# A graph layer kernel: a reordered head, and ring chunks taken in turn with others in the third unit

## The chip, the cores and the metric

One core of one Trainium2 chip runs the kernel. The metric is the device time of one execution in microseconds (us), as the median of several runs.

## The reference

There are 256 nodes with 1024 features and 8448 edges (66 tiles of 128). What matters of it:

```
h = relu(layernorm(x))
feat = concat(h[src], h[dst])              # 8448 x 2048
e = relu(feat @ W_kind + b_kind)           # kind hh: tile 0; oo: tiles 1 to 5; ho: the other 60
logit = e @ W_a + b_a
alpha = softmax of logit over the edges with the same dst
z = segment_sum(alpha * h[src], dst)
x1 = x + relu(concat(h, z) @ W_hn or W_on + bias)     # rows 0..63 use hn, the others on
out = x1 + relu(layernorm(x1)) @ W.T + l1_bias        # W scattered from edge_weight at (src, dst)
```

## The kernel before

**Units.** For the ho edges the kernel doesn't multiply 8448 rows: it makes the tables p_ho = h @ top and q_ho = h @ bottom (256 rows each), stores them in HBM and gathers one row of each per edge. The work on TensorE (PE) is in units of 8 chunks; a chunk is 128 rows of a weight matrix (512 KB). Units 0 and 1 (p_ho, q_ho) are the split units: each chunk is rounded to a high half Wh (ScalarE, ACT, L423) and a remainder Wl (VectorE, DVE, L633), h transposed likewise to hTh (ACT, L455) and hTl (DVE, L639), and `split_chunk` (L858 to L873) makes three products per row tile and column half: hTh by Wh, hTh by Wl, hTl by Wh, 12 matmuls per chunk. Then comes the hh unit (L972 to L998): 16 chunks against hsT, the gathered rows of tile 0. The other units (tables oo, then on and hn) are jobs (L1000 on) of one chunk or a pair each, dealt out between the lots by PACE.

**Lots.** Edge tiles go in lots of mostly 3. Per tile, POOL gathers a row block of p into Gp (12 slots) and one of q into Gq (8 slots); DVE adds them (`total`, L682), makes two onehots (L673, L675) and the logit (L686); ACT makes weight products RW (L490) and logit products RL (L500); PE counts edges (psC in psB, and psW) and places logits (psA), both at L918. The onehot ring has 9 slots, so DVE's tenth onehot after the early ones waits for the first placed tile (L670).

**The head.** SP loads x in two tiles (L258), the ids, and five weight chunks. DVE takes the statistics, ACT makes h (L414) for each row tile and then issues the store of h_rows (L417), from which tile 0's rows are gathered (L364). PE waits for the constants, then transposes h (L845). It holds hTh and hTl, Wh and Wl of the chunk complete before it starts a chunk's first product (L858, with the wait for s_hTl before even chunks). POOL clears `zero` last of its memsets (L348).

**Order of the weights.** SP issues ring loads (W, 5 slots) in order: while q-5 is in the split units, load q waits for its remainder; afterwards it waits on the chunk that used the slot (`uses_before`, L95). The first 11 chunks of the hh unit do not lie in the ring but in buffers that are free then: pre_f (3), pre_l (2, the place of RL), Gq slots 4 to 7, and two parts of T. Its chunks 11 to 15 lie in the five ring slots and are used last. So the ring's next load (q = 21) waits for the twelfth hh chunk, and the gathers into Gq slots 4 to 7 wait for the chunks there (L389).

```
            for c in range(2):
                for k in range(KC):
                    n = c * KC + k
                    q = SPLIT + n - PRE
```

Of the kernel before, what the change touches and what calls it, by code (L numbers as in the profile page):

```python
# [44 lines left out]
HALVES = 4  # L45
NP = 12
# [14 lines left out]
TOPS = SPLIT + HH - PRE + PLAIN  # L61
CHUNKS = TOPS + 2 * KC
# [32 lines left out]
def uses_before(q):  # L95

    gone = q - WSLOTS
    if gone < SPLIT:
        return gone + 1
    return gone + PRE + 1 if gone < TOPS else TOPS + PRE + (gone - TOPS) // 2 + 1  # L100


def gnn_block(nc, x, edge_ids, edge_w, weights, bias_rows, w_a, b_a, l1_bias, out):
# [13 lines left out]
    with ctx:  # L117
# [95 lines left out]
        s_x = [sem(f"x_in{t}") for t in range(NT)]  # L213
# [42 lines left out]
        def _(sp):  # L256
            for t in range(NT):
                sp.dma_start(xs[:, t, :], by_tile(x)[:, t, :]).then_inc(s_x[t], 16)  # L258
# [82 lines left out]
        def _(pool):  # L341
            nc.gpsimd.memset(epst[:, :], EPS).then_inc(s_eps, 1)
            nc.gpsimd.memset(minus[:, :], -1.0)
# [4 lines left out]
            nc.gpsimd.memset(zero[:, :], 0.0)  # L348
# [9 lines left out]
                                    pattern=[[-1, BIASES]], channel_multiplier=1).then_inc(s_const, 1)  # L358
            pool.wait_ge(s_ids, 16)
# [47 lines left out]
        def _(act):  # L407
            act.wait_ge(s_eps, 1)
            nc.scalar.activation(warm[:, :], epst[:, :], ACT.Sqrt)
            for t in range(NT):  # L410
# [41 lines left out]
            for b in range(4):  # L452
                highs(b, b + 1)
# [40 lines left out]
            def logit_product(g, i, half, val):  # L494
# [3 lines left out]
                elif half == 0:  # L498
                    act.wait_ge(s_wused, SPLIT + PRE_HEAD)
# [96 lines left out]
        def _(dve):  # L596
# [11 lines left out]
            def half_stats(t, b):  # L608
                chain(nc.vector.bn_stats(st[:, t, b, :], xs[:, t, b * HALF:(b + 1) * HALF]))
# [10 lines left out]
            dve.wait_ge(s_x[0], 16)  # L620
# [3 lines left out]
            dve.wait_ge(s_x[1], 16)  # L624
# [4 lines left out]
            norm(1)  # L629

            def low(q):
                dve.wait_ge(s_hi, q + 1)
# [205 lines left out]
        def _(pe):  # L838
            pe.wait_ge(s_const, 1)
            for t in range(NT):  # L840
                pe.wait_ge(s_h, t + 1)
                for b in range(4):
                    for i in range(2):
# [41 lines left out]
            for k in range(KC):  # L885
                if k % 2 == 0:
                    pe.wait_ge(s_hTl, k // 2 + 1)
# [81 lines left out]
            for c in range(2):  # L969
                for k in range(KC):  # L970
                    n = c * KC + k
                    q = SPLIT + n - PRE  # L972
                    if n < PRE:
                        pe.wait_ge(s_pre[n], 16)
                    else:
                        chunk_in(q)
                    rows = pre[n] if n < PRE else W[:, q % WSLOTS, :]
                    for half in range(2):
                        last = nc.tensor.matmul(psG[:, half, :], hsT[:, c, k, :], rows[:, half * HALF:(half + 1) * HALF],  # L979
                                                start=False, stop=c == 1 and k == KC - 1, skip_group_check=True)  # L980
                    last.then_inc(s_wused, 1)
                    i = n - 2
                    if 0 <= i < len(EARLY):
                        count(i, EARLY[i:i + 1])
                    elif i == 6:
                        lot_count(0)
                    elif i == 8:
                        lot_count(1)
                    elif i == 9:
                        lot_place(0)  # L990
# [194 lines left out]
```

## Time and profile before

| | us |
|---|---|
| median of 3 runs (326.26 to 327.69) | 326.42 |
| the profiled execution's own time | 328.05 |
| its span, first to last instruction | 326.2 |
| PE busy | 304.4 (93%) |
| DVE busy | 254.3 (78%) |
| ACT busy | 175.9 (54%) |
| POOL busy | 155.1 (48%) |
| moved by DMA | 122.06 MB, mean 374 GB/s |
| granted TensorE clock, mean | 0.989 |

Busy PE is modelled from starts and counts overlapping instructions once; "issue" is time in which an engine waits for nothing that the profile shows; "remote" is a releaser that the profile could not name. A float32 matmul of 128x512 appears as two instructions.

### The profile page before, as it was taken

What the parts mean: (1) busy time and instruction counts of PE and PEld (TensorE: products, weight loads), DVE (VectorE), ACT (ScalarE), POOL (GpSimd) and SP (SyncE); (2) the same over time, 40 slices, a digit from 0 to 9 for tenths busy, and PEclk for the clock granted to TensorE, in tenths of its full rate; (3) what the DMA queues carried; (4) which work ended last, traced back from release to release, by engine and by line L of the source; (5) the groups of instructions that cost most, each with busy time, mean ns of one, the idle gap of its engine ahead of it and who ended that gap; (6) DMA issues with size and microseconds to landing.
All of it is one profiled execution on the core that took longest, in us unless ns stands there. A gap on an engine that the chain in (4) does not pass through costs nothing.

```text
span 326.2 us, 4198 instructions
## 1 busy us (share of the span) xinstructions
PE 304.4 (93%) x1381; PEld 194.7 (60%) x1381; DVE 254.3 (78%) x446; ACT 175.9 (54%) x437; POOL 155.1 (48%) x148
## 2 busy tenths in 40 slices
PE   0899999999958999999999999999989989999995
PEld 0687688755634756665766675575645554456543
DVE  4657437303992998999989999999999999986444
ACT  3873451372461586277874465576438398562202
POOL 3040048307784877657766658578777720000000
PEclk9999999999996999999999999999999999999999
DMA  7999999998999999999999999999999999999304
GB/s 263 404 403 410 407 377 395 409 418 324 346 390 370 384 413 408 409 410 408 411 417 408 409 410 410 405 418 410 409 408 411 409 407 409 406 407 410 110 0 129
DMA packets 34425, 122.06 MB, mean 374 GB/s; under 512 B 4058, under 2 KB 4570, under 8 KB 34404
## 3 DMA queue, kind: packets, MB, share of 16 engines
q0 software_dynamic: 19008, 69.21, 53.7%
q1 hardware_dynamic: 14004, 47.34, 37.5%
q10 hardware_dynamic: 1392, 5.24, 3.9%
q8 instruction: 11, 0.18, 0.2%
q14 instruction: 10, 0.08, 0.1%
HBM read 115.49 MB, written 6.29 MB: 373 GB/s over the span
## 4 chain that ended last, share of the span: by engine, by line
PE 59%; DVE 25%; ACT 8%; issue 5%; another core or an unknown queue 2%; DMA 1%; ACTq 0%; DVEq 0%
PE psG L868 13%; PE psG L1010 11%; PE psG L979 9%; DVE Gp L686 7%; DVE Gp L682 7%; PE psA L918 6%; PE psW L918 6%; PE psB L918 3%; PE psG L1032 3%; ACT RL L500 3%; DVE ohd L675 2%; PE psG L1087 2%; DVE inv_few L728 2%; PE psG L1040 2%
## 5 line engine op out<-in xcount | busy, mean ns | idle before, releaser
L379 POOL DMA_INDIRECT Gp<-p_ho,ids x60 | 66.7, 1112 | 55.2 <-DMA p_ho<-T 24.2
L682 DVE TENSOR_TENSOR Gp<-Gp,Gq 128x1024 f32<-128x1024 f32 x65 | 79.2, 1218 | 15.9 <-DMA Gq<-q_ho,ids 15.9
L393 POOL DMA_INDIRECT Gq<-q_ho,ids x60 | 70.3, 1172 | 34.1 <-issue 17.4
L1010 PE MATMUL psG<-W,hT 128*128 128x512 f32 x192 | 84.9, 592 | 0.0
L686 DVE SCALAR_TENSOR_TENSOR Gp<-Gp,wa 128x1024 f32<-128x1024 f32 x65 | 79.1, 1217 | 0.4
L1010 PEld LDWEIGHTS psG<-W,hT 128*128 128x128 f32 x192 | 35.3, 190 | 39.1 <-issue 39.1
L490 ACT ACTIVATE RW<-ohs,ewh 128x256 fp32r<-128x256 f32 x66 | 33.2, 504 | 41.9 <-DVE ohs L673 29.3
L918 PE MATMUL psW<-RW,ohd 128*128 128x256 f32 x264 | 44.4, 290 | 0.0
L918 PE MATMUL psA<-RL,ohd 128*128 128x256 f32 x240 | 36.2, 289 | 7.6 <-issue 4.8
L918 PEld LDWEIGHTS psA<-RL,ohd 128*128 128x128 f32 x240 | 31.1, 190 | 13.5 <-issue 7.2
L918 PEld LDWEIGHTS psW<-RW,ohd 128*128 128x128 f32 x264 | 36.3, 189 | 3.0 <-issue 2.9
L633 DVE TENSOR_TENSOR Wl<-W,Wh 128x1024 fp32r<-128x1024 f32 x16 | 19.6, 1223 | 20.2 <-ACT Wh L423 20.2
L673 DVE TENSOR_SCALAR ohs<-iota,idf 128x256 fp32r<-128x256 f32 x72 | 26.3, 365 | 9.7 <-remote 8.5
L500 ACT ACTIVATE RL<-ohs,lg 128x256 fp32r<-128x256 f32 x66 | 32.9, 499 | 0.0
L500 ACT ACTIVATE RL<-ohs,lgl 128x256 fp32r<-128x256 f32 x66 | 32.7, 495 | 0.1
L490 ACT ACTIVATE RW<-ohs,ewl 128x256 fp32r<-128x256 f32 x66 | 32.7, 496 | 0.0
L918 PE MATMUL psB<-ohs,ohd 128*128 128x256 f32 x132 | 31.8, 328 | 0.0
L918 PEld LDWEIGHTS psB<-ohs,ohd 128*128 128x128 f32 x132 | 20.9, 189 | 10.4 <-issue 10.0
L675 DVE TENSOR_SCALAR ohd<-iota,idf 128x256 fp32r<-128x256 f32 x72 | 25.6, 356 | 0.0
L423 ACT CAST Wh<-W 128x1024 fp32r<-128x1024 f32 x16 | 16.8, 1052 | 16.0 <-PE psG L868 15.0
L868 PE MATMUL psG<-Wh,hTh 128*128 128x512 f32 x64 | 20.5, 402 | 1.4 <-DVE hTl L639 1.4
L868 PE MATMUL psG<-Wl,hTh 128*128 128x512 f32 x64 | 19.8, 391 | 0.0
(180 smaller groups left out, 360.5 us busy)
## 6 DMA issues: line engine op xcount, KB each, us to landing
W<-weights SPq DMA_DIRECT2D x61, 512.0 KB, 13.9
Gp<-weights SPq DMA_DIRECT2D x8, 512.0 KB, 10.1
Gq<-weights SPq DMA_DIRECT2D x4, 512.0 KB, 10.8
pre_f<-weights SPq DMA_DIRECT2D x3, 512.0 KB, 6.7
xs<-x SPq DMA_DIRECT2D x2, 512.0 KB, 3.7
h_rows<-h ACTq DMA_DIRECT2D x1, 1024.0 KB, 6.5
pre_l<-weights SPq DMA_DIRECT2D x2, 512.0 KB, 9.3
p_ho<-T ACTq DMA_DIRECT2D x2, 512.0 KB, 6.5
```

The source lines that it names most:

```text
L379: nc.gpsimd.indirect_dma_start(out=Gp[:, i % NP, :], out_offset=None, in_=p_oo if t <= OO_TILES else p_ho, in_offset=bass.IndirectOffsetOn ...
L393: nc.gpsimd.indirect_dma_start(out=Gq[:, i % NQ, :], out_offset=None, in_=q_oo if t <= OO_TILES else q_ho, in_offset=bass.IndirectOffsetOn ...
L490: last = nc.scalar.activation(RW[:, w % WRING, half, :], ohs[:, (first + i) % RING, :].bitcast(f32), ACT.Copy, scale=val[:, t:t + 1].bitca ...
L500: return nc.scalar.activation(RL[:, n % LRING, half, :], ohs[:, (ENTRY[g] + i) % RING, :].bitcast(f32), ACT.Copy, scale=val[:, g % 2, i:i ...
L673: nc.vector.tensor_scalar(ohs[:, n % RING, :], iota[:, :], idf[:, tile, 0:1], None, ALU.is_equal).then_inc(s_ohs, 1)
L675: nc.vector.tensor_scalar(ohd[:, n % RING, :], iota[:, :], idf[:, tile, 1:2], None, ALU.is_equal).then_inc(s_ohd, 1)
L682: nc.vector.tensor_tensor(Gp[:, i % NP, :], Gp[:, i % NP, :], Gq[:, i % NQ, :], ALU.add).then_inc(s_sum, 1)
L686: nc.vector.scalar_tensor_tensor(out=Gp[:, i % NP, :], in0=Gp[:, i % NP, :], scalar=0.0, in1=wa[:, :], op0=ALU.max, op1=ALU.mult, accum_ou ...
L868: ins = nc.tensor.matmul(psG[:, 2 * t + half, :], lhs[:, k, cols], rhs[:, s, half * HALF:(half + 1) * HALF], start=not opened and k == 0 a ...
L918: ins = nc.tensor.matmul(bank[:, c, :], ohd[:, slot, c * P:(c + 1) * P], m, start=False, stop=False, skip_group_check=True)
L979: last = nc.tensor.matmul(psG[:, half, :], hsT[:, c, k, :], rows[:, half * HALF:(half + 1) * HALF], start=False, stop=c == 1 and k == KC - ...
L1010: last = nc.tensor.matmul(psG[:, 2 * t + half, :], hT[:, k, t * P:(t + 1) * P], W[:, s, half * HALF:(half + 1) * HALF], start=u != 1 and k ...
```

## The change

It changes six things.

1. x is loaded as four DMAs of half a row tile each, and each statistics instruction waits for its half alone.
2. PE runs 12 matmuls of zeros (WARM) into psG before it waits for the constants; POOL clears `zero` right after its first memset, for that.
3. h of the second row tile: ACT makes columns 0 to 511, DVE the others in two instructions. The store of h_rows moves from ACT's queue to SP's, behind the first loads and the bias rows, with waits for both parts.
4. The high halves of weight chunks 0 and 1 are made by POOL (POOL_HIGHS), before its cast of the ids; ACT makes those from 2 on.
5. `split_chunk` waits for Wh and hTh at its start, for Wl before the first product with it, and for hTl before the first with that.
6. The hh unit takes its chunks as 3, 4, 11, 5, 12, 6, 13, 7, 14, 8, 15, 9, 10, 0, 1, 2. The waits of the ring, of RL, of Gq slots 4 to 7 and of `few_counts` are put on the matching steps. Counts and the first placement stay at the same steps of the unit.

```diff
+HH_ORDER = [3, 4] + [11, 5, 12, 6, 13, 7, 14, 8, 15] + [9, 10] + [0, 1, 2]
+HH_USED = {n: SPLIT + i + 1 for i, n in enumerate(HH_ORDER)}
...
+    if gone < SPLIT + HH - PRE:
+        return HH_USED[PRE + gone - SPLIT]
...
             for t in range(NT):
-                sp.dma_start(xs[:, t, :], by_tile(x)[:, t, :]).then_inc(s_x[t], 16)
+                for half in range(2):
+                    cols = slice(half * HALF, (half + 1) * HALF)
+                    sp.dma_start(xs[:, t, cols], by_tile(x)[:, t, cols]).then_inc(s_x[t][half], 16)
...
             sp.dma_start(bar[:, :], b_a.broadcast_to((P, 1))).then_inc(s_small, 16)
+            sp.wait_ge(s_h, NT)
+            sp.wait_ge(s_hd, 1)
+            sp.dma_start(by_tile(h_rows), h[:, :, :]).then_inc(s_hst, 16)
...
+            nc.gpsimd.memset(zero[:, :], 0.0).then_inc(s_zero, 1)
...
+            for q in range(POOL_HIGHS):
+                pool.wait_ge(s_w[q], 16)
+                nc.gpsimd.tensor_copy(Wh[:, q, :], W[:, q, :]).then_inc(s_hip, 1)
             pool.wait_ge(s_ids, 16)
...
-                    pool.wait_ge(s_wused, SPLIT + PRE_HEAD + i - HALVES + 1)
+                    pool.wait_ge(s_wused, HH_USED[PRE_HEAD + i - HALVES])
...
-                nc.scalar.activation(h[:, t, :], xs[:, t, :], ACT.Relu, bias=nb[:, t:t + 1],
+                cols = slice(0, (D, HALF)[t])
+                nc.scalar.activation(h[:, t, cols], xs[:, t, cols], ACT.Relu, bias=nb[:, t:t + 1],
                                      scale=rs[:, t:t + 1]).then_inc(s_h, 1)
-            act.wait_ge(s_h, NT)
-            act.dma_start(by_tile(h_rows), h[:, :, :]).then_inc(s_hst, 16)
...
-                highs(b, b + 1)
+                if b >= POOL_HIGHS:
+                    high(b)
...
-                    act.wait_ge(s_wused, SPLIT + PRE_HEAD)
+                    act.wait_ge(s_wused, max(HH_USED[3], HH_USED[4]))
...
+            chain(nc.vector.tensor_scalar(h[:, 1, HALF:D], xs[:, 1, HALF:D], rs[:, 1:2], nb[:, 1:2], ALU.mult, ALU.add))
+            nc.vector.tensor_scalar(h[:, 1, HALF:D], h[:, 1, HALF:D], 0.0, None, ALU.max).then_inc(s_hd, 1)
...
-                dve.wait_ge(s_wused, SPLIT + 2)
+                dve.wait_ge(s_wused, SPLIT + HH)
...
+            pe.wait_ge(s_zero, 1)
+            for _ in range(WARM):
+                nc.tensor.matmul(psG[:, 0, :], zero[:, 0:P], zero[:, :], start=True, stop=True, skip_group_check=True)
             pe.wait_ge(s_const, 1)
...
+                    if t == NT - 1 and b == 2:
+                        pe.wait_ge(s_hd, 1)
...
-                pe.wait_ge(s_lo, q + 1)
+                if q < POOL_HIGHS:
+                    pe.wait_ge(s_hip, q + 1)
+                else:
+                    pe.wait_ge(s_hi, q - POOL_HIGHS + 1)
+                pe.wait_ge(s_hTc, k // 2 + 1)
...
+                        if t == 0 and n == 1:
+                            pe.wait_ge(s_lo, q + 1)
+                        elif t == 0 and n == 2:
+                            pe.wait_ge(s_hTl, k // 2 + 1)
...
-            for c in range(2):
-                for k in range(KC):
-                    n = c * KC + k
-                    q = SPLIT + n - PRE
+            for step, n in enumerate(HH_ORDER):
+                c, k = divmod(n, KC)
+                q = SPLIT + n - PRE
```

## Rows read from the trace of the kernel before

**Rows 1.** The page: busy share of each engine, and DMA in 40 slices of the span.

```profile
PE 304.4 (93%) x1381; PEld 194.7 (60%) x1381; DVE 254.3 (78%) x446; ACT 175.9 (54%) x437; POOL 155.1 (48%) x148
...
DMA  7999999998999999999999999999999999999304
```

**Rows 2.** Timeline of the head (start us, us, engine, line, what), to the last h.

```profile
0.74 0.86 SPq L258 DMA_DIRECT2D xs<-x  x2
...
4.01 1.42 DVE L609 BATCH_NORM_STATS2 st<-xs 128x6 f32<-128x512 f32 x2 [4.01 <-DMA xs<-x]
...
6.66 1.24 ACT L414 ACTIVATE h<-xs,nb,rs 128x1024 f32<-128x1024 f32 x1 [0.66 <-DVE nb L617]
...
8.51 1.24 ACT L414 ACTIVATE h<-xs,nb,rs 128x1024 f32<-128x1024 f32 x1 [0.42 <-DVE nb L617]
```

**Rows 3.** Timeline, the work of the first weight chunk and of the first hT bank.

```profile
10.22 1.05 ACT L423 CAST Wh<-W 128x1024 fp32r<-128x1024 f32 x1 [0.47 <-ACT h L414]
...
11.17 0.58 ACT L455 CAST hTh<-psB 128x512 fp32r<-128x512 f32 x1
...
11.30 1.22 DVE L633 TENSOR_TENSOR Wl<-W,Wh 128x1024 fp32r<-128x1024 f32 x1 [2.82 <-ACT Wh L423]
...
12.44 0.68 DVE L639 TENSOR_TENSOR hTl<-psB,hTh 128x512 fp32r<-128x512 f32 x1
```

**Rows 4.** The chain that ended last: first products of the split unit.

```profile
13.18 13.91 PE psG L868 x60
```

**Rows 5.** Groups by line in 0 to 45 us: the nearest prices (mean ns).

```profile
L845 PE MATMUL psB<-ident,h 128*128 128x128 f32 x8 | 2.2, 431 | 8.0 <-ACT h L414 8.0
...
L908 PE MATMUL psB<-ident,hs 128*128 128x128 f32 x8 | 1.2, 271 | 0.0
...
L347 POOL MEMSET brow<- 64x1024 f32 x1 | 1.0, 956 | 0.0
...
L360 POOL CAST idf<-ids 128x132 f32<-128x132 int32 x1 | 0.3, 293 | 2.5 <-DMA ids<-edge_ids 2.5
```

**Rows 6.** Windows: busy time of each engine, granted clock, DMA share, GB/s.

```profile
0.00:7.00 7.00, 0.00 (x0) 0.00 (x0) 2.85 (x7) 2.12 (x4) 3.11 (x16) 1.00 0.75 241
...
75.00:80.00 5.00, 5.00 (x20) 2.68 (x18) 1.09 (x1) 0.47 (x2) 3.78 (x5) 1.00 0.79 309
...
85.00:115.00 30.00, 24.99 (x108) 16.21 (x107) 23.45 (x42) 15.36 (x44) 20.56 (x19) 0.89 1.01 376
...
130.00:262.00 132.00, 129.90 (x588) 81.35 (x586) 129.40 (x226) 77.65 (x216) 92.13 (x80) 1.00 1.03 410
```

**Rows 7.** Timeline of POOL and SP between the two gather waves.

```profile
73.40 0.94 POOL L393 DMA_INDIRECT Gq<-q_ho,ids  x1 [12.35 <-DMA q_ho<-T]
...
83.02 1.00 POOL L393 DMA_INDIRECT Gq<-q_ho,ids  x1 [0.41 <-PE psG L979]
...
103.51 6.29 SPq L262 DMA_DIRECT2D W<-weights  x5
```

**Rows 8.** The chain that ended last, hh unit, and where PE crawls.

```profile
70.09 1.72 PE psG L979 x4
...
71.81 0.47 PE psW L918 x4
...
92.69 0.28 PE psA L918
...
101.09 8.36 PE psG L979 x16
```

**Rows 9.** Timeline of DVE: its first sum, and its longest idle time after it.

```profile
78.91 1.23 DVE L682 TENSOR_TENSOR Gp<-Gp,Gq 128x1024 f32<-128x1024 f32 x1 [15.88 <-DMA Gq<-q_ho,ids]
...
103.65 0.35 DVE L673 TENSOR_SCALAR ohs<-iota,idf 128x256 fp32r<-128x256 f32 x1 [6.55 <-remote]
```

**Rows 10.** The end: DVE's wait for x (timeline), and the chain beside it.

```profile
307.01 0.69 DVE L806 SCALAR_TENSOR_TENSOR x<-psG,x 128x512 f32<-128x512 f32 x1 [2.51 <-DMA x<-x]
...
308.40 5.15 PE psG L1087 x24
```

More of the change, by code:

```diff
@@ L45 @@
 HALVES = 4
+POOL_HIGHS = 2
+WARM = 12
 NP = 12
@@ L61 @@
 TOPS = SPLIT + HH - PRE + PLAIN
+HH_ORDER = [3, 4] + [11, 5, 12, 6, 13, 7, 14, 8, 15] + [9, 10] + [0, 1, 2]
+HH_USED = {n: SPLIT + i + 1 for i, n in enumerate(HH_ORDER)}
+assert sorted(HH_ORDER) == list(range(HH))
 CHUNKS = TOPS + 2 * KC
@@ L211, in gnn_block @@
         hT_banks = [psB[:, 0, :], psB[:, 1, :], whole(psA), whole(psW)]
-        s_x = [sem(f"x_in{t}") for t in range(NT)]
+        s_x = [[sem(f"x_in{t}{half}") for half in range(2)] for t in range(NT)]
+        s_zero, s_hip, s_hd = sem("zero_made"), sem("first_w_high_made"), sem("h_last_half_made")
         s_ids, s_ew, s_wa, s_small = map(sem, ("ids_in", "ew_in", "wa_in", "small_in"))
@@ L347, in _ @@
             nc.gpsimd.memset(brow[:, :], 0.0).then_inc(s_pool, 1)
-            nc.gpsimd.memset(zero[:, :], 0.0)
             nc.gpsimd.iota(iota[:, :], pattern=[[1, N]], base=0, channel_multiplier=0,
@@ L608, in half_stats @@
             def half_stats(t, b):
+                dve.wait_ge(s_x[t][b], 16)
                 chain(nc.vector.bn_stats(st[:, t, b, :], xs[:, t, b * HALF:(b + 1) * HALF]))
@@ L618, in norm @@
                                                op0=ALU.mult, op1=ALU.mult).then_inc(s_nb, 1)
-            dve.wait_ge(s_x[0], 16)
             half_stats(0, 0)
@@ L623, in _ @@
             variance(0)
-            dve.wait_ge(s_x[1], 16)
             half_stats(1, 0)
@@ L629, in _ @@
             norm(1)
+            dve.wait_ge(s_nb, NT)
+            chain(nc.vector.tensor_scalar(h[:, 1, HALF:D], xs[:, 1, HALF:D], rs[:, 1:2], nb[:, 1:2], ALU.mult, ALU.add))
+            nc.vector.tensor_scalar(h[:, 1, HALF:D], h[:, 1, HALF:D], 0.0, None, ALU.max).then_inc(s_hd, 1)
             def low(q):
-                dve.wait_ge(s_hi, q + 1)
+                if q < POOL_HIGHS:
+                    dve.wait_ge(s_hip, q + 1)
+                else:
+                    dve.wait_ge(s_hi, q - POOL_HIGHS + 1)
                 nc.vector.tensor_tensor(Wl[:, q % HALVES, :], W[:, q % WSLOTS, :], Wh[:, q % HALVES, :].bitcast(f32),
@@ L860, in split_chunk @@
             def split_chunk(q, k, opened):
-                pe.wait_ge(s_lo, q + 1)
+                if q < POOL_HIGHS:
+                    pe.wait_ge(s_hip, q + 1)
+                else:
+                    pe.wait_ge(s_hi, q - POOL_HIGHS + 1)
+                pe.wait_ge(s_hTc, k // 2 + 1)
                 s = q % HALVES
@@ L885, in _ @@
             for k in range(KC):
-                if k % 2 == 0:
-                    pe.wait_ge(s_hTl, k // 2 + 1)
                 split_chunk(k, k, False)
@@ L968, in _ @@
             bias(1, everyone, 0, 1)
-            for c in range(2):
-                for k in range(KC):
-                    n = c * KC + k
-                    q = SPLIT + n - PRE
[L973 to L990, printed above, removed]
+            for step, n in enumerate(HH_ORDER):
+                c, k = divmod(n, KC)
+                q = SPLIT + n - PRE
+                if n < PRE:
+                    pe.wait_ge(s_pre[n], 16)
+                else:
+                    chunk_in(q)
+                rows = pre[n] if n < PRE else W[:, q % WSLOTS, :]
+                for half in range(2):
+                    last = nc.tensor.matmul(psG[:, half, :], hsT[:, c, k, :], rows[:, half * HALF:(half + 1) * HALF],
+                                            start=False, stop=step == HH - 1, skip_group_check=True)
+                last.then_inc(s_wused, 1)
+                i = step - 2
+                if 0 <= i < len(EARLY):
+                    count(i, EARLY[i:i + 1])
+                elif i == 6:
+                    lot_count(0)
+                elif i == 8:
+                    lot_count(1)
+                elif i == 9:
+                    lot_place(0)
             def job(j):
```

## The prediction

> **What bounds the kernel now.** I read the page first. PE is busy 93% of the span and the DMA engines stand at 9 tenths in nearly every slice [rows 1]: two resources are full at once, and DVE is the third. The windows say it more closely: from 130 to 262 us PE works 129.9 of 132 us, DVE 129.4, and DMA has a share of 1.03 at 410 GB/s [rows 6]. In that stretch nothing can be gained by reordering; a gain must come from before it, and it must bring all three forward.
>
> Before it there are three losses. First, the head: h is made from 6.66 and 8.51 us on [rows 2], and the first real product starts at 13.18 [rows 4]. Second, PE crawls from 92.69 to 101.09: the 12 matmuls of the first placement take 8.4 us [rows 8], and DVE stands idle for 6.55 us until 103.65 because its onehot needs the first placed tile [rows 9]; the ring's next load also goes out only at 103.51 [rows 7]. The profile names no wait of PE there. Third, DMA runs dry at 75 to 80 us (share 0.79, 309 GB/s), and while only gathers are queued it gives 376 GB/s in 85 to 115 us rather than 410 [rows 6].
>
> **x in four.** The whole first tile lands 4.01 - 0.74 = 3.3 us after its issue [rows 2]. Its first half holds 256 KB, 0.64 us less of transfer at 410 GB/s [rows 6], so DVE's first statistics start 0.6 us sooner and the second follows; h0 then starts near 6.0 instead of 6.66. Two more issues of 0.43 us each (0.86 us for two [rows 2]) push the first weight loads on SP back by 0.9 us. That I cost at nothing: the x, ids and W0 bytes (1.64 MB) need until 7.0 us at the 241 GB/s of the window 0 to 7 [rows 6], so W0 stands in the DMA queue anyway; without that cover it is 0.9 us.
>
> **h split between ACT and DVE.** Second tile: ACT's 1.24 us [rows 2] become about 0.65; DVE takes two 128x512 instructions. There is no such row; bounds are 0.3 us (a quarter of the 1.22 us for 128x1024 with two inputs [rows 3]) and 0.7 us (the 0.68 of hTl [rows 3]); I take 0.45, as one input is read. So h is whole at about 7.85 + 0.95 = 8.8 instead of 8.51 + 1.24 = 9.75.
>
> **The warm-up.** The early transposes take 431 ns, later ones of the same shape 271 ns [rows 5]: PE runs at the lower of its two levels (1.2 GHz) after having done nothing for 8 us, though the clock column shows 1.00. Twelve matmuls of 512 columns, at twice the 13.91 / 60 = 0.23 us of the full level [rows 4], fill 5.6 us from about 1.5 us on, to 7.1: before h0 is there (7.2), so they delay nothing. The 8 transposes of the second tile then need about 1 us rather than 2. First bank ready at 8.8, hTh of it (0.58 [rows 3]) at 9.4.
>
> **POOL makes two high halves.** POOL has no 128x1024 cast in the trace. Below: 0.96 us, its memset of 1024 columns; above: 0.293 x 1024 / 132 = 2.3 us, its only cast scaled up [rows 5]. I take 1.6, the cast with some 0.1 us of fixed time taken off. From W0's landing at about 7.2 they run to 8.8 and 10.4. ACT loses two casts of 1.05 us that stood ahead of hTh [rows 3].
>
> **Products of high halves first.** PE starts at 9.5 with hTh by Wh. Then Wl of chunk 0 (DVE, 1.22) is ready at 8.9 + 1.2 = 10.1, hTl (0.68) at 10.8 [rows 3]. Two of the 12 matmuls are done by then and perhaps two more; the other 8 take 8 x 0.23 = 1.9 us: chunk 0 ends at 12.7. Before it ends at 13.18 + 12 x 0.23 = 15.9. Gain 3.2 us.
>
> The rows show no POOL read beside a DVE instruction with two inputs in SBUF. Bounds: no delay, or DVE's first Wl waits for the end of POOL's second copy (10.4) and chunk 0 ends at 14.2, gain 1.7 us. The Trainium skill, page "SBUF — State Buffer", section "Who interferes with whom", says that a VectorE instruction with two SBUF inputs and a GpSimd instruction that reads SBUF block each other, whichever starts first holding the port; by it the lower gain, 1.7 us, is the one to take. POOL's second copy begins at the same moment as Wl 0 can, so either may win; I take 3.0 us and keep 1.7 for the range.
>
> Later chunks keep it. DVE needs 1.22 + 0.68 = 1.9 us per chunk and bank, PE 2.76; W lands in time, for 4 chunks of Wh lie ahead of PE. The h_rows store on SP holds up only loads that need Wl 0 anyway, and its gathered rows are first used in unit 1. POOL's later cast of the ids is wanted only by the onehots, which stand on DVE behind all sixteen remainders. Were that cover gone, it would be POOL's 3.2 us.
>
> **The hh order.** No instruction is added. A chunk costs 1.72 us and a tile's counts 0.47 [rows 8]. The unit starts near 64.3 - 3.0 = 61.3. The ring's slots come free after steps 3, 5, 7, 9 and 11, so five loads (2.6 MB, 6.4 us of DMA) go out between 67 and 86 us instead of from 103.51 on [rows 7]. They fill the hole at 75 to 80 (0.21 x 5 = 1.05 us). Against it: Gq slot 7 comes free with step 10, at 61.3 + 10 x 1.72 + 6 x 0.47 + 2.1 = 83.4 (2.1: three tiles of lot 0, each 0.47 for psW and half as much for psC), while POOL issues that gather at 83.02 now [rows 7]. POOL's queue holds behind it all later gathers, which therefore go out as now, 0.4 us later; DVE comes to that tile only 7 tiles after its first sum, each with 1.23 for the sum, the like for the logit and 0.35 for a onehot, pipelined near 2.8: about 98. So that costs nothing. Job 0 will find its chunk landed, but PE shows no wait there now. So I cost this part at 0 on the chain, with 1 us gained by DMA.
>
> **The sum.** PE reaches the first placement at 92.7 - 3.0 = 89.7. The logits it needs come from DVE, whose first sum stands at 78.91 [rows 9] even if the gathers do not come sooner; lot 0's products are then ready from 89 on (three tiles and 1.6 us on ACT). If the crawl keeps its 8.4 us, DVE's wait, the next lots and everything until the end go 3.0 us earlier: 328.05 - 3.0 = 325.05 for the profiled execution. Its own time is 1.63 us over the median, so the median becomes 326.42 - 3.0 = 323.4. Does DMA allow it? x lands at 307.01 now; its readers must be done when the hn rows end after 308.40 + 5.15 = 313.55 [rows 10], and new_rows with its statistics needs twice 0.69 us: 5.1 us of slack, plus the 1 us from the hole. Three fit.
>
> **Rivals.**
> (a) **The crawl goes.** It may depend on what else stands in the queues at 92 to 103 us: only gathers are there then, and after the change the ring loads are done and DVE is as far as before. If it goes, DVE gains its 6.55 us [rows 9] and PE 3.0 and most of the 8.4; DMA's slack of 6.1 us then decides: 326.4 - 6.1 = 320.3. For it: no row gives the crawl a cause inside PE. Against: nothing in the edit touches it.
> (b) **DMA takes the head's gain.** DMA is full from 2 us on, and the first q gather had to wait for the q_ho store in it until 73.40 [rows 7]; the bytes ahead of it are the same, plus two ring loads. If the later stages hang on DMA at 410 GB/s, only the 1 us of the hole is won: 325.5, within noise of 326.4. For it: share 1.03 throughout. Against: DVE never waits for a gather after its first.
> (c) **The edit does less than it says:** port or slow POOL copies leave 1.7 us or none: 325.
> (d) **Slower.** The five ring loads now run ahead of the first q gathers. They can delay DVE's first sum by their 6.4 us, and slot 7's wait may add to it. The idle 6.55 us at 97 to 103.65 absorb that; it decides only once the first sum comes after 78.91 + 6.55 = 85.5 us. With another 2 us of wait for slot 7 the time is 326.4 + 2 = 328.4.
>
> **How the numbers follow.** Forecast, 323.4: 0.42, own range 322 to 324.9. (a) 0.23. (b) and (c) together 0.23. (d) 0.12. A difference of 0.5% (1.6 us) is about what a measurement of this kernel tells from none. Faster: 0.41 of the forecast, (a), and 0.02 of (c): 0.66. Same: 0.22. Slower: 0.12. The range reaches from 318.8, where (a) also wins DMA's whole slack and its rate beside gathers, to 327.2, which leaves out most of (d).
>
> **What would show it.** First L868 matmul at 9.5 us and not 13.18; chunk 0's end near 12.7 (14.2 if the port blocks); Wl 0 right beside POOL's copies. The hh unit starting near 61.3. Ring loads between 67 and 86 us and a window 75 to 80 with a share near 1. POOL's eighth q gather near 83.4. DVE's first sum at 76 to 79. The crawl still there, 3 us earlier, and DVE's release near 100.6. I am wrong if PE is at 61.3 but DVE's release is not before 103, or if the last x lands after 312.

## The result, and the profile after

| | us, median (lowest to highest) | runs |
|---|---|---|
| before | 326.07 (324.97 to 328.35) | 13 |
| after | 324.21 (322.88 to 327.01) | 13 |

The ratio is 0.9946, with a 95% interval of 0.9922 to 0.9970: faster by about 0.5%, at the edge of what the prediction called measurable. By medians that is 1.9 us, and the forecast was 3.0. The profiled execution took 323.78 us with a span of 322.0, 4.3 us less than that of before (328.05 and 326.2). So the two traces show more than the medians; the first experiment says why. In the table of the experiments the ratios and their intervals leave out runs in a slower state (two of r9, three of r10, two of r11, one of r12 and one of the kernel before on that chip), while the medians hold all runs.

The page of after, with the engines' busy time, the DMA engines' tenths, and the share of each engine in the chain that ended last:

```profile
PE 308.8 (96%) x1388; PEld 195.8 (61%) x1393; DVE 256.2 (80%) x448; ACT 174.2 (54%) x435; POOL 156.7 (49%) x150
...
DMA  6999999999999999999999999999999999999604
...
DMA 29%; PE 21%; DVE 20%; POOL 18%; issue 9%; ACT 2%; SPq 1%; ACTq 0%; DVEq 0%
```

The same line of the page of before, the chain:

```profile
PE 59%; DVE 25%; ACT 8%; issue 5%; another core or an unknown queue 2%; DMA 1%; ACTq 0%; DVEq 0%
```

PE was 59% of the chain in that profile, and now DMA has the largest part. The edit did not do this: a second profile of the kernel before (r1 below) has PE 26%, DMA 24%, DVE 20%.

The timeline of the head, after:

```profile
3.45 0.69 DVE L628 BATCH_NORM_STATS2 st<-xs 128x6 f32<-128x512 f32 x1 [3.45 <-DMA xs<-x]
...
6.48 1.24 ACT L433 ACTIVATE h<-xs,nb,rs 128x1024 f32<-128x1024 f32 x1 [0.72 <-DVE nb L636]
...
8.91 0.43 DVE L649 TENSOR_SCALAR h<-h 128x512 f32<-128x512 f32 x1
9.07 3.33 POOL L376 CAST Wh<-W 128x1024 fp32r<-128x1024 f32 x2 [5.53 <-DMA W<-weights]
...
10.26 1.22 DVE L656 TENSOR_TENSOR Wl<-W,Wh 128x1024 fp32r<-128x1024 f32 x1 [0.93 <-POOL Wh L376]
...
10.40 0.70 PE L904 MATMUL psG<-Wh,hTh 128*128 128x512 f32 x2
11.41 0.68 DVE L662 TENSOR_TENSOR hTl<-psB,hTh 128x512 fp32r<-128x512 f32 x1
```

h of the first tile starts at 6.48 instead of 6.66 [rows 2], and the first product at 10.40 instead of 13.18 [rows 4]. Chunk 0 ends near 14.1; the prediction had worked out 15.9 for before. W0 is late: POOL waits for it until 9.07. POOL's two copies stand as one line of 3.33 us, 9.07 to 12.40, and DVE's Wl 0 lies inside it, from 10.26 to 11.48. A copy took 1.04 us in later kernels where it began before DVE's instruction (r8, r12); so the second of this pair was held up.

Windows of after (columns as in [rows 6]):

```profile
34.00:41.00 7.00, 6.05 (x19) 4.19 (x19) 2.35 (x3) 1.66 (x3) 0.00 (x0) 0.76 1.03 414
37.00:38.00 1.00, 1.00 (x4) 0.81 (x3) 0.88 (x1) 0.09 (x1) 0.00 (x0) 0.50 1.02 406
75.00:80.00 5.00, 5.00 (x18) 2.67 (x18) 0.70 (x1) 0.57 (x2) 3.78 (x5) 1.00 1.02 364
85.00:115.00 30.00, 29.75 (x135) 18.94 (x134) 30.00 (x54) 20.83 (x59) 22.04 (x20) 1.00 0.99 372
130.00:262.00 132.00, 128.24 (x577) 80.96 (x578) 125.48 (x219) 82.55 (x227) 94.22 (x81) 0.99 1.03 410
```

The stretch 75 to 80 is fuller than before (364 GB/s instead of 309), and 130 to 262 runs at the same 410 GB/s [rows 6]. PE's clock is lost at the seam of the two split units, at its lower level (0.50, 1.2 GHz) from 37 to 38. Before, PE has 1.00 there. It stood idle at 34 to 36.3, in bits (0.38 us waiting for DVE and 0.57 us for ACT), before the clock fell. Of the eight other profiles with the new head two lose it there too (r5 at 0.76 and r12 at 0.86 in 34 to 41 us).

The first and the eighth q gather on POOL, after:

```profile
73.33 0.93 POOL L411 DMA_INDIRECT Gq<-q_ho,ids  x1 [13.43 <-DMA q_ho<-T]
...
87.16 1.44 POOL L411 DMA_INDIRECT Gq<-q_ho,ids  x1 [4.17 <-PE psG L1012]
```

The first starts as before (73.40 [rows 7]), the eighth 4.1 us later than before, after an idle 4.17 us.

PE after, at the start of the hh unit and at the first placement:

```profile
64.30 3.70 PE L1012 MATMUL psG<-pre_l,hsT 128*128 128x512 f32 x8
...
91.87 1.98 PE L952 MATMUL psA<-RL,ohd 128*128 128x256 f32 x12
```

The 12 matmuls of the first placement take 1.98 us. The crawl of [rows 8] is gone, and so is DVE's idle 6.55 us of [rows 9]. In its place, DVE after:

```profile
79.30 1.22 DVE L705 TENSOR_TENSOR Gp<-Gp,Gq 128x1024 f32<-128x1024 f32 x1 [16.72 <-DMA Gq<-q_ho,ids]
...
159.64 1.22 DVE L705 TENSOR_TENSOR Gp<-Gp,Gq 128x1024 f32<-128x1024 f32 x1 [1.44 <-DMA Gq<-q_ho,ids]
...
286.22 1.22 DVE L705 TENSOR_TENSOR Gp<-Gp,Gq 128x1024 f32<-128x1024 f32 x1
...
306.01 0.69 DVE L829 SCALAR_TENSOR_TENSOR x<-psG,x 128x512 f32<-128x512 f32 x1 [5.79 <-DMA x<-x]
```

DVE waits for gathers here, at nine of its sums between 159 and 279 us; one of them is shown. In the first profile of before it waited only at its first. The sum of the last tile stands at 286.22, against 287.72 there. DVE had been 8.2 us ahead of that trace at its seventeenth sum (124.63 against 132.81), and at the last it was 1.5. Most of the 8.2 us is the crawl of that one profile, not the edit: in r1 the seventeenth sum stands at 125.88, 1.3 us behind after, and DVE waits for gathers as well. So time won back from the crawl does not arrive at the last sum, because DVE then waits for rows. The last x lands for DVE's use at 306.01, before the 312 that was to show the prediction wrong.

### The profile page after: what moved, and what is told of

Same layout as the page of the kernel before. It is cut to its first block, busy times and chain, and to the rows that moved or that the text cites. A ratio compares the mean times of both kernels' runs of the same rounds, so it can differ in the third digit from the quotient of the medians.

```text
span 322.0 us, 4235 instructions
## 1 busy us (share of the span) xinstructions
PE 308.8 (96%) x1388; PEld 195.8 (61%) x1393; DVE 256.2 (80%) x448; ACT 174.2 (54%) x435; POOL 156.7 (49%) x150
## 4 chain that ended last, share of the span: by engine, by line
DMA 29%; PE 21%; DVE 20%; POOL 18%; issue 9%; ACT 2%; SPq 1%; ACTq 0%; DVEq 0%
DMA Gq<-q_ho,ids 14%; POOL Gp L397 10%; POOL Gq L411 8%; PE psG L904 7%; DMA W<-weights 7%; DMA Gq<-q_oo,ids 7%; DVE Gp L705 5%; PE psG L1012 5%; DVE Gp L709 5%; DVE inv_few L751 2%; PE psG L1120 2%; PE psW L952 1%; DVE ohd L698 1%; PE psG L1115 1%; DVE Wl L656 1%
## 5 line engine op out<-in xcount | busy, mean ns | idle before, releaser
L397 POOL DMA_INDIRECT Gp<-p_ho,ids x60 | 70.6, 1177 | 47.5 <-DMA p_ho<-T 24.2
L411 POOL DMA_INDIRECT Gq<-q_ho,ids x60 | 66.0, 1100 | 40.4 <-issue 16.8
L1043 PEld LDWEIGHTS psG<-W,hT 128*128 128x128 f32 x192 | 35.7, 192 | 39.6 <-issue 39.1
L952 PE MATMUL psA<-RL,ohd 128*128 128x256 f32 x240 | 37.0, 296 | 3.6 <-ACT RL L518 2.7
L952 PEld LDWEIGHTS psW<-RW,ohd 128*128 128x128 f32 x264 | 36.3, 189 | 2.9 <-issue 2.9
L440 ACT CAST Wh<-W 128x1024 fp32r<-128x1024 f32 x14 | 14.6, 1054 | 18.1 <-PE psG L904 8.9
L904 PE MATMUL psG<-Wh,hTh 128*128 128x512 f32 x64 | 21.3, 415 | 0.1
```

Of the source, the lines that this page charges most:

```text
L397: nc.gpsimd.indirect_dma_start(out=Gp[:, i % NP, :], out_offset=None, in_=p_oo if t <= OO_TILES else p_ho, in_offset=bass.IndirectOffsetOn ...
L411: nc.gpsimd.indirect_dma_start(out=Gq[:, i % NQ, :], out_offset=None, in_=q_oo if t <= OO_TILES else q_ho, in_offset=bass.IndirectOffsetOn ...
L904: ins = nc.tensor.matmul(psG[:, 2 * t + half, :], lhs[:, k, cols], rhs[:, s, half * HALF:(half + 1) * HALF], start=not opened and k == 0 a ...
L952: ins = nc.tensor.matmul(bank[:, c, :], ohd[:, slot, c * P:(c + 1) * P], m, start=False, stop=False, skip_group_check=True)
L1043: last = nc.tensor.matmul(psG[:, 2 * t + half, :], hT[:, k, t * P:(t + 1) * P], W[:, s, half * HALF:(half + 1) * HALF], start=u != 1 and k ...
```

## The experiments

All were timed beside the kernel before on the same chip. Runs 1 to 4 share one chip (before: 326.25, 35 runs), 5 to 8 a second (325.93, 11 runs), 9 to 12 a third (326.85, 35 runs).

| kernel | median us | ratio to before (95%) | hh unit starts | last sum | span |
|---|---|---|---|---|---|
| r1 before, again | 325.87 | 0.9995 (0.9969 to 1.0022) | 65.91 | 288.03 | 323.8 |
| r2 head only | 324.47 | 0.9955 (0.9926 to 0.9983) | 63.25 | 285.39 | 321.1 |
| r3 order only | 325.36 | 0.9979 (0.9948 to 1.0009) | 66.43 | 289.55 | 325.3 |
| r4 busy gap | 324.36 | 0.9961 (0.9933 to 0.9988) | 64.42 | 288.77 | 324.5 |
| r5 after, more bytes | 329.64 | 1.0112 (1.0080 to 1.0143) | 64.64 | 294.14 | 329.9 |
| r6 before, more bytes | 331.71 | 1.0181 (1.0147 to 1.0216) | 64.39 | 292.42 | 328.2 |
| r7 after, half rows | 330.03 | 1.0116 (1.0079 to 1.0153) | 62.98 | 292.40 | 328.1 |
| r8 slots first | 321.94 | 0.9882 (0.9856 to 0.9909) | 62.34 | 284.21 | 320.0 |
| r9 slots, old head | 326.50 | 0.9972 (0.9937 to 1.0008) | 65.70 | 287.83 | 324.6 |
| r10 slots, no warm-up | 325.13 | 0.9956 (0.9925 to 0.9987) | 62.77 | 284.72 | 321.8 |
| r11 slots, ACT's highs | 323.83 | 0.9902 (0.9871 to 0.9934) | 62.39 | 285.36 | 322.6 |
| r12 slots, ids later | 325.97 | 0.9972 (0.9938 to 1.0006) | 66.23 | 286.88 | 324.1 |

The last three columns are of the one profiled execution. In the first profiles these are 64.20, 287.72 and 326.2 for before, and 64.30, 286.22 and 322.0 for after. The kernel after itself was not timed again on any of the three chips.

**r1: the kernel before, once more.** No edit.

> The kernel before, unchanged, profiled once more. Theory A (the crawl of PE at the first placement belongs to the old order): a stretch of some 8 us again in which the 12 psA matmuls are spread out and VectorE idles over 5 us, with ScalarE's copy of the hh unit near 109 us. Theory B (the crawl is a chance event of one execution): no such stretch, the hh unit ends near 101, and the time is within 0.3% of the other runs of this kernel, since the DMA engines then set the end.

PE at the first placement, ACT's first work on the denominators, and DVE's Z, in this second profile of the same kernel:

```profile
93.47 1.98 PE L918 MATMUL psA<-RL,ohd 128*128 128x256 f32 x12
...
286.34 0.67 ACT L526 ACTIVATE inv<-psB,minus 128x512 f32<-128x512 f32 x1
...
292.84 0.42 DVE L770 TENSOR_TENSOR Z<-psA,inv 128x256 f32<-128x256 f32 x1
```

The last two in the first profile of before:

```profile
288.72 0.69 ACT L526 ACTIVATE inv<-psB,minus 128x512 f32<-128x512 f32 x1 [2.60 <-PE psW L918]
...
295.31 0.42 DVE L770 TENSOR_TENSOR Z<-psA,inv 128x256 f32<-128x256 f32 x1 [2.33 <-PE psA L918]
```

The crawl does not belong to the code: here the 12 matmuls take 1.98 us, with the same kernel. DVE's last sum is at 288.03, not earlier than with the crawl (287.72), because DVE then waits for gathers as in the profile of after. But PE doesn't catch up what it lost: in the first profile ACT waits 2.60 us for psW and DVE 2.33 us for the last psA, and from the last sum to the end of the span it is 326.2 - 287.72 = 38.5 us, here 323.8 - 288.03 = 35.8. So this profile's tail is 2.7 us longer, more than the 2.0 us by which the first profile's execution lies over the median of before. Taken against r1, the profile of after is 288.03 - 286.22 = 1.8 us earlier at the last sum and 1.8 us in span: the same as the medians' 1.9.

The two profiles of one kernel differ in another place. Their hh units start at 64.20 and 65.91, 1.7 us apart and long before the crawl. In r1 the first matmuls of the split unit ran at half rate:

```profile
13.36 1.22 PE L868 MATMUL psG<-Wh,hTh 128*128 128x512 f32 x2 [1.40 <-DVE hTl L639]
...
14.38 1.06 PE L868 MATMUL psG<-Wl,hTh 128*128 128x512 f32 x2
```

Such a pair starts 0.45 us after the one before it once PE is at full rate; here it is 0.85 to 1.0 us, for the first seven matmuls. The clock column shows 1.00 all the same. r3 and r9, which also have the old head, show the same; the first profile of before and r6 do not. So a start of the hh unit that is read from one profile is uncertain by 1.7 us, as much as what the head is said to gain.

The hole in DMA is wider here than in the first profile:

```profile
75.00:80.00 5.00, 5.00 (x19) 2.73 (x18) 0.00 (x0) 0.91 (x2) 3.59 (x4) 1.00 0.63 219
80.00:85.00 5.00, 5.00 (x22) 2.97 (x22) 4.54 (x8) 1.04 (x3) 3.60 (x5) 1.00 0.71 288
```

**r2: the head alone.** The hh unit keeps its old order.

```diff
-HH_ORDER = [3, 4] + [11, 5, 12, 6, 13, 7, 14, 8, 15] + [9, 10] + [0, 1, 2]
+HH_ORDER = list(range(HH))
```

> The head as changed, hh chunks in the old order. Theory A (order carries the gain): within 0.5 us of the kernel before; first product near 10.4 us but the hh unit starts at 64, since the clock falls at the gap between the two split units, or the p and q stores wait in the DMA queue. Theory C (the head carries it, as predicted): 2 us or more faster.

Windows of r2, and the timeline of PE and DVE at the hh unit's start and the first sum:

```profile
34.00:41.00 7.00, 6.43 (x28) 4.47 (x27) 2.89 (x4) 2.74 (x5) 0.00 (x0) 1.00 1.03 413
75.00:80.00 5.00, 5.00 (x22) 3.01 (x21) 2.17 (x4) 0.64 (x2) 3.96 (x4) 1.00 0.87 341
```

```profile
63.25 5.42 PE L1012 MATMUL psG<-pre_f,hsT 128*128 128x512 f32 x12
...
77.83 1.23 DVE L705 TENSOR_TENSOR Gp<-Gp,Gq 128x1024 f32<-128x1024 f32 x1 [16.31 <-DMA Gq<-q_ho,ids]
```

The head alone gives as much as both parts, within the noise: 0.9955, where both give 0.9946. In this execution (322.96 us, 1.5 under the kernel's median; r1's 325.61 is 0.3 under its own) the clock stays at 1.00 at the seam, and the 2.7 us by which the hh unit starts before r1's stand nearly unchanged at the first sum (80.46 - 77.83 = 2.6), at the last (2.6) and in the span (2.7). So what the hh unit is ahead does reach the end. How much of the 2.7 us is the head's is less sure, since r1 had lost 1.5 us to slow first matmuls; by medians of the two it is 325.87 - 324.47 = 1.4 us.

**r3: the order alone.** The old head, with change 6 only.

> The old head, hh chunks in the new order. Theory A: 1.5 to 2 us faster than the kernel before, ring loads from 69 us on, no crawl. Theory C: within 0.5 us of the kernel before.

POOL's eighth q gather in r3:

```profile
89.29 1.79 POOL L400 DMA_INDIRECT Gq<-q_ho,ids  x1 [4.97 <-PE psG L985]
```

Nothing measurable is gained (0.9979, the interval holds 1; it also overlaps with r2's, so the head is told from before and the order isn't, but the two are not told from each other). The hole at 75 to 80 is filled, yet from 85 to 115 DMA gives 371 GB/s, where r1 gave 406. POOL stands 4.97 us for Gq slot 7, and every later gather stands behind it.

**r4: PE kept busy at the seam.** The bias rows of the second split unit get seven matmuls of zeros between them.

```diff
+            def zeros(times):
+                for _ in range(times):
+                    nc.tensor.matmul(psB[:, 1, :], zero[:, 0:P], zero[:, :], start=True, stop=True, skip_group_check=True)
+
...
-            bias(0, everyone, 0, 0)
-            bias(0, everyone, 2, 0)
+            for bank, spare in ((0, 2), (1, 3), (2, 0), (3, 2)):
+                free(bank, 0)
...
+                zeros(spare)
```

> The changed kernel with 7 matmuls of zeros in the gaps of PE between the two split units (into a bank that is free then), so that its clock does not fall there. Their product is used nowhere. If the head's gain is lost to the clock alone, the hh unit starts 1.5 us sooner, near 62.8, and the time falls by up to 1.5 us. If DMA bounds what follows, the unit starts sooner but the first q gather stays at 73 us and the time within 0.5 us of the changed kernel's.

The window at the seam:

```profile
34.00:41.00 7.00, 7.00 (x29) 4.03 (x29) 3.01 (x4) 1.80 (x3) 0.00 (x0) 1.00 1.03 413
```

The clock holds at 1.00 where it had been 0.76, and the time stays that of after (0.9961 and 0.9946). The hh unit starts at 64.42, as in after (64.30): in this execution the first product came only at 11.58, so one loss took the place of the other. That leaves open what the clock at the seam costs in the median. The late start is in its head:

```profile
9.50 1.14 DVE L649 TENSOR_SCALAR h<-h 128x512 f32<-128x512 f32 x1
...
10.52 1.04 POOL L376 CAST Wh<-W 128x1024 fp32r<-128x1024 f32 x1 [0.16 <-DMA W<-weights]
10.56 2.07 DVE L656 TENSOR_TENSOR Wl<-W,Wh 128x1024 fp32r<-128x1024 f32 x1
```

DVE's second instruction on h took 1.14 us, beside POOL's first copy, instead of 0.43, and began 0.6 us later than in after; so h was whole at 10.64 instead of 9.34, and the first product came 1.2 us later. Then POOL's second copy began 0.04 us before Wl 0, and Wl 0 took 2.07 us instead of 1.22.

**r5 and r6: more bytes.** Four more copies of 512 KB from HBM to HBM, on SP's queue, in the kernel after and in the one before.

```diff
                 load(q)
+                if q in (30, 33, 36, 39):
+                    n = (q - 30) // 3
+                    sp.dma_start(spare_rows[n * P:(n + 1) * P, :], weights[q * P:(q + 1) * P, :]).then_inc(s_spare, 16)
```

> The changed kernel with 4 further transfers of 512 KB each (2.1 MB, weight rows to a spare place in HBM, read by nobody), issued by SP behind the ring loads 30, 33, 36 and 39, in the middle of the run. Theory DMA (after the head the DMA engines set the end): 2.1 MB at 410 GB/s is 5.1 us, and the time grows by 4 to 6 us over the changed kernel's 324.2. Theory PE and DVE (they set the end, DMA has slack of 6 us): under 1 us more.

> The same 4 transfers in the kernel before. Theory DMA: also 4 to 6 us over its 326.2. Theory PE and DVE: under 1 us more.

The 2.1 MB take 2.1 / 0.410 = 5.1 us at the full rate. After costs 1.0112 / 0.9946, 1.7% or 5.4 us more; before costs 1.8% or 5.9 us more. Both kernels pay for added bytes at about DMA's full rate: both hang on DMA in the middle, though the first profile of before showed not one wait for a gather there. The added copies go from HBM to HBM and stand in SP's queue ahead of later ring loads; that they cost what gathered rows would is argued.

**r7: fewer bytes.** The q gathers of tiles 20 to 27 fetch 64 rows in place of 128.

```diff
-                nc.gpsimd.indirect_dma_start(out=Gq[:, i % NQ, :], out_offset=None, in_=q_oo if t <= OO_TILES else q_ho,
+                rows = slice(0, P // 2 if 20 <= i < 28 else P)
+                nc.gpsimd.indirect_dma_start(out=Gq[rows, i % NQ, :], out_offset=None,
...
```

> The changed kernel, where the q gathers of the eight tiles 20 to 27 fetch 64 of 128 rows (the other 64 keep what the slot held, so those edges' logits are not the reference's). 2.1 MB less, every instruction stays. Theory DMA: VectorE's waits for Gq between tiles 44 and 61 go, and the last sum comes up to 5.1 us sooner until PE or DVE bind: 2 to 5 us faster than the changed kernel. Theory PE and DVE: under 0.5 us.

A miss: it is slower than after, by 1.0116 / 0.9946 or 1.7%. DMA's page of the stretch 130 to 150, first after, then r7 (the second line is POOL's queue: packets, MB, share of 16 engines' time):

```profile
DMA packets 2223, 8.17 MB, mean 409 GB/s; under 512 B 232, under 2 KB 232, under 8 KB 2221
...
q0 software_dynamic: 1669, 6.08, 76.2%
```

```profile
DMA packets 1572, 5.59 MB, mean 280 GB/s; under 512 B 211, under 2 KB 211, under 8 KB 1570
...
q0 software_dynamic: 1037, 3.65, 69.7%
```

With 2.1 MB less to move, the engines are as busy and bring 280 GB/s in place of 409. Per MB, POOL's queue takes 69.7 / 3.65 = 19 points of share, before the cut 76.2 / 6.08 = 12.5. The Trainium skill, page "SBUF — State Buffer", section "Door 1: The DMA port swizzle", says that the partitions 0 to 63 reach only half of the ports that all 128 reach. Worked out from that, as an estimate, half the rows take as long as all, and the run would be no faster; the fall in rate agrees, but the 5.5 us of loss are more than it says, and are not explained. So no run shows what fewer bytes would give at an unchanged rate.

**r8: the Gq slots first.** Each chunk in a Gq slot is used one step before the ring chunk that it alternates with.

```diff
-HH_ORDER = [3, 4] + [11, 5, 12, 6, 13, 7, 14, 8, 15] + [9, 10] + [0, 1, 2]
+HH_ORDER = [3, 4] + [5, 11, 6, 12, 7, 13, 8, 14, 15] + [9, 10] + [0, 1, 2]
```

> The changed kernel with the hh chunks 3, 4, 5, 11, 6, 12, 7, 13, 8, 14, 15, 9, 10, 0, 1, 2: each Gq slot before the ring chunk beside it. GpSimd's eighth q gather goes out near 82.6 instead of 87.2 us. If that gather and those queued behind it matter, the time falls by up to 1.5 us; if DMA's bytes alone set the end, within 0.5 us of the changed kernel's.

Windows and the eighth q gather in r8:

```profile
75.00:80.00 5.00, 5.00 (x19) 2.78 (x18) 1.32 (x2) 0.00 (x0) 3.99 (x4) 1.00 1.03 411
85.00:115.00 30.00, 28.57 (x131) 18.27 (x130) 30.00 (x54) 21.27 (x60) 23.43 (x22) 1.00 1.03 409
```

```profile
81.16 1.22 POOL L411 DMA_INDIRECT Gq<-q_ho,ids  x1 [0.44 <-PE psG L1012]
```

POOL's wait for slot 7 falls from 4.17 us to 0.44, and DMA gives 409 to 411 GB/s in both stretches; no window from 60 to 262 us falls below 408. Its 321.94 is the lowest time of the study, below both kernels: the interval, 0.9856 to 0.9909, lies apart from that of after. It rests on six runs, and after was timed on another chip, so the two are compared only by their ratios to before.

**r9 to r12: parts of r8.** r9 has r8's order with the old head. r10 is r8 without the warm-up (WARM = 0), r11 with all high halves on ACT (POOL_HIGHS = 0), r12 with the load of the ids moved behind those of the first five weight chunks.

> The kernel before with the order of r8 (each Gq slot before the ring chunk beside it) and its old head. If the order's gain is that DMA is never short of work from 60 us on, the windows 75 to 115 us stand at 405 GB/s or more and the time is 1.5 to 3 us under the kernel before; the head then adds the rest of r8's 4. If r8's gain needs the new head, it is under 1 us.

> r8 without the 12 matmuls of zeros at the start. The prediction's reason: transposes of the second tile take 1 us more and the first chunk runs at half speed, so the hh unit starts 1 to 3 us later and the time grows by 1 to 2 us. If DMA alone sets the end and keeps its order, under 0.5 us.

> r8 with all high halves on ScalarE, as before the change. If POOL's two copies and VectorE's remainders block each other for about 1 us and so eat what they save, the time stays within 0.5 us of r8. If the copies carry the head, ScalarE's 1.05 us per copy ahead of hTh costs 1 to 2 us.

> r8 with the load of the edge ids moved behind the first five weight chunks. Weight chunk 0 landed at 9.0 us in the changed kernel, not at 7.2 as predicted, and the first product waits for it. If the ids' small pieces hold it up, it lands 0.5 to 1 us sooner and the time falls by up to 1 us; if not, nothing changes.

r9 isn't told from before. So the better order alone isn't shown to gain, as r3's wasn't. In its profile POOL still waits 1.06 us for a slot, at 84.51.

r11 holds up nearly all of r8's gain: its first product comes at 10.96, against 10.72, and its ratio, 0.9902, overlaps with r8's 0.9882. POOL's copies bring nothing that these runs can tell. r10 has a first product at 11.02 and the hh unit at 62.77, 0.4 us behind r8, but its ratio, 0.9956, lies 0.7% above r8's. The profile shows 1.8 us of that in span. r8 was timed on another chip, though, and r10's interval overlaps with that of r11, its neighbour on the same chip; so what the warm-up is worth isn't told apart. r12 has W0 1.0 us sooner (7.96), but POOL's first copy then fell on DVE's small instruction for nb, which took 0.98 us instead of 0.16, DVE's second half of h took 1.14 us beside the other copy, PE's first product came at 11.59 and the clock in 7 to 20 us was 0.74; the hh unit started at 66.23 and nothing was gained.

r11 also shows the crawl again, with a different head and order. DVE's wait in it, its Z, and the chain's shares on the page; then the same wait in r9:

```profile
110.47 0.35 DVE L696 TENSOR_SCALAR ohs<-iota,idf 128x256 fp32r<-128x256 f32 x1 [5.06 <-remote]
...
291.61 0.43 DVE L793 TENSOR_TENSOR Z<-psA,inv 128x256 f32<-128x256 f32 x1 [1.57 <-PE psA L952]
```

```profile
PE 76%; DVE 13%; ACT 4%; issue 4%; DMA 1%; SPq 0%; ACTq 0%; DVEq 0%
```

```profile
122.85 0.35 DVE L680 TENSOR_SCALAR ohs<-iota,idf 128x256 fp32r<-128x256 f32 x1 [6.28 <-remote]
```

As in the first profile of before, DVE is released by something unnamed, PE then has the largest share of the chain (76%), DVE waits for the last psA (1.57 us), and from the last sum to the end it is 322.6 - 285.36 = 37.2 us, not 35.8. r10's profile has such a wait too (4.90 us, at 118.70) and a tail of 37.1, and so has r12's (4.86 us, at 122.01; tail 37.2); r9's tail is 36.8. In all four, as in the first profile of before, DVE never waits for a gather after its first sum.

So all four profiles of the third chip have the crawl, and none of the eight of the other two (tails 35.7 to 35.8). It comes with either head and either order, at different places between 93 and 123 us. Whether it is chance in each execution or something of the chip isn't shown; on which chip the first two profiles were taken isn't known.

## Why the prediction was right and wrong

The direction, the interval and the size of a modest gain held: 324.2 lies in 318.8 to 327.2. The forecast's gain, 3.0 us, measured 1.9. That the head carries the gain, and that what it gains reaches the end, was right: the hh unit starts at 65.3 us on the mean of the five profiles with the old head (before, r1, r3, r6, r9) and at 63.5 on the mean of seven with the new head and the warm-up (after, r2, r4, r5, r7, r8, r11), 1.9 us sooner; with r12, the worst, and r10 it is 1.6. In part the number is luck. The prediction worked from the one profile of before, and against that one nothing is left of the 3.0 us at the start of the hh unit (64.30 against 64.20). It also took the crawl to stay, and the profile of after has none. Step by step:

**x in four, and h split.** The first statistics started 0.56 us sooner (0.6 said). h0 came at 6.48, not 6.0: 0.18 us gained. h was whole at 9.34, not 8.8. DVE's two instructions took 0.55 and 0.43 us for 0.45 each.

**The warm-up.** It filled 1.36 to 6.15, and the transposes ran faster, four of them in 0.66 us where the same four took 1.11 us before. r10, without it, has the first product 0.3 us later than r8, and its first pair of matmuls takes 1.20 us instead of 0.71. The kernels with the old head, which have no warm-up, lose about 1.5 us to slow first matmuls in three profiles of five (r1, r3, r9), those with the warm-up in one of eight (r12). The prediction counted only the transposes; the rest of the profit lies here, and the profile that it was made from hid it.

**POOL's high halves.** This is the first step that failed. I had W0 landing at 7.2; it landed at 9.0. The two more issues of x had been costed at nothing, with W0 standing in DMA's queue anyway. SP issued W0 at 3.07 instead of 2.12, and the queue wasn't full. The window 0 to 9, after and then before:

```profile
0.00:9.00 9.00, 5.85 (x20) 2.45 (x20) 4.41 (x12) 3.88 (x6) 2.83 (x15) 1.00 0.71 244
```

```profile
0.00:9.00 9.00, 0.95 (x5) 0.98 (x6) 3.62 (x10) 3.69 (x6) 3.11 (x16) 1.00 0.81 277
```

DMA's share is 0.71 for 0.81, and by 9 us it had moved 9 x 33 = 297 KB less, 0.7 us of transfer. So of the 1.9 us by which W0 is late I put about half down to SP, and the rest to the bytes of other loads; r12, where W0 is ahead of the ids and lands 1.0 us sooner, agrees with that. The copy itself was cheaper, 1.04 us for 1.6 where it began first, and 1.17 here. By both, Wh 0 was ready at 10.24 instead of 8.8.

**Products of high halves first.** First product 10.40 (9.5 said), Wl 0 at 10.26 to 11.48, hTl at 11.41 to 12.1, chunk 0's end near 14.1. The gain is 1.8 us where I took 3.2 with no block and 1.7 with it. The ends of the range were right and the choice between them wrong. POOL and DVE do hold each other up. In after and r8 DVE began first or with it, and POOL's second copy took about 2.1 us. In r4 POOL began first, and DVE took 2.07. This timeline of r8 shows both ways, for DVE's two-operand and its one-operand instruction:

```profile
8.94 1.04 POOL L376 CAST Wh<-W 128x1024 fp32r<-128x1024 f32 x1 [5.40 <-DMA W<-weights]
9.10 1.15 DVE L649 TENSOR_SCALAR h<-h 128x512 f32<-128x512 f32 x1
...
10.18 1.21 DVE L656 TENSOR_TENSOR Wl<-W,Wh 128x1024 fp32r<-128x1024 f32 x1
10.22 2.08 POOL L376 CAST Wh<-W 128x1024 fp32r<-128x1024 f32 x1 [0.24 <-DMA W<-weights]
```

DVE's maximum with one input, 0.43 us in after, takes 1.15 beside POOL's copy. The Trainium skill, page "SBUF — State Buffer", section "Who interferes with whom", says that an instruction of VectorE with two SBUF inputs and one of GpSimd that reads SBUF shut each other out, and that a tensor_scalar in a two-port mode does so too. The traces agree, with those numbers. I named this rule and took the other value; 1.7 was the one to take.

**"Later chunks keep it."** The second step that failed, in the profiled execution. The hh unit started at 64.3, not at 61.3: against r1's 65.91 only 1.6 us were left. The 12 matmuls at the seam took 4.47 us instead of 2.94, at the lower clock level, after PE had stood idle in bits. I had looked for cover of DVE and ACT, and not asked what PE waits for where two units meet, with W landing no sooner than before. ACT now waited 7.9 us for W in four waits between 14 and 64 us. r2 and r8, with 63.25 and 62.34, lose nothing there: they are 2.7 to 3.6 us ahead of r1, but 0.9 to 1.9 us ahead of the first profile, whose first matmuls ran at full rate.

**The hh order at 0.** The sum was right and its terms were not. I gave DMA 1 us from the hole and slot 7 no price. The hole was worth more (219 and 288 GB/s in two windows of r1), but with the eighth gather at 87.16, where 83.4 was said, DMA fell to 372 GB/s for 85 to 115. (The sum for slot 7 was sound: with the unit at 64.30 instead of 61.3 it gives 86.4.) Nor was the low rate a matter of gathers alone, as I had read from the first profile: in r1 DMA gave 411 and 407 GB/s in 85 to 90 and 90 to 95, before the ring's next load at 94.07. "So that costs nothing" looked at DVE's need of tile 7. What was to be asked is what DMA has left to do while POOL's queue stands; the ring loads that could have filled it had already gone. r3 measured the sum of both, nothing that its noise tells; r8 took the wait away and kept the rate at 409. That the wait is the whole cause of the fall is argued: after has 334 GB/s again in 110 to 115.

**Rival (b)** holds in its premise, DMA sets the middle (r5, r6), but not in its consequence: the gain wasn't taken, as r2 shows. In its profile the whole stream of gathers starts sooner with the head (first q gather at 72.32, against 75.49 in r1 and 73.40 in the first profile), which I had not counted on. I had "DVE never waits for a gather after its first" against it. That was read in an execution with a crawl, in which PE was late instead.

**Rival (a)** named the right thing, the crawl, as independent of the edit. But it isn't removed by the change; it comes and goes between profiles of either kernel. Its place in the time is the tail, 2.7 us longer in the first profile and 1.0 to 1.4 in the four of the third chip, and not 6.1: the last sum is no earlier without DVE's 6.55 idle us.

**Rival (c)** came true in part (the port). **Rival (d)**, slower, had its mechanism, the wait for slot 7, at 4.2 us and not 2; but the ring loads didn't delay the first sum (79.30), and the point of 85.5 us was far off.

Open: what holds PE and DVE up in the crawl, and whether it goes with the chip; what starts PE's first matmuls at half rate in one execution and not in another; why r10 and r12 have less of r8's gain than the profiles show; and why r7 loses and doesn't stay even. That the ratio of r8 would repeat on another chip wasn't tried; r11 is the nearest to it, and its interval overlaps with that of after too. So the gain of r8 over after rests on r8 alone.

## What to carry to other kernels

Profile a kernel more than once, and on more than one chip, before a stall or a start goes into a sum: a stall that the second profile lacks is not the change's to win, and it can hide other waits (here for gathers). Two profiles of one kernel put the start of a unit 1.7 us apart, while the whole change was worth 1.9. Where DMA's share is full, add some bytes and see whether the time follows at the full rate; a full share says that the engines are occupied, not that they move bytes at the best rate. And when buffers are reordered, price each wait by the whole queue behind it: the same order with four pairs exchanged took POOL's wait from 4.2 us to 0.4.

## What the runs showed of the hardware that was not expected

- A matmul stream can crawl for about 8 us with no releaser in the trace, in one profile of a kernel and not in another (first profile of before: 12 matmuls in 8.4 us; r1: 1.98 us). All four profiles of the third chip have such a stall, none of the eight of the other two.
- The first matmuls of a stream can run at half rate while the clock column shows 1.00 (r1: a pair takes 1.22 us, in the first profile of before 0.72).
- Gathers into 64 partitions brought DMA down to 280 GB/s at a share of 1.03, where those into 128 gave 409.
- POOL's cast of 128x1024 takes 1.04 us when it begins first and 2.08 when a DVE instruction with two inputs in SBUF does; DVE's 1.22 becomes 2.07 when POOL is first, and its 0.43 for 128x512 with one input becomes 1.15.
